# A relational graph layer on one core: root weight loaded early, features permuted early, basis parts in fours

## The reference, cut to what matters

```python
edge_index = jnp.stack([src, dst])
# layer 0: x @ W.T, normalised aggregation over edges, batch norm, GELU, + x
x = _layernorm(x + _L0_gnn_ref(x, edge_index, W, b, gamma, beta))
# layer 1, twice (relu between): w[r] = sum_b att[r,b] * basis[b]  (30 bases of 512x512)
w = jnp.einsum('rb,bio->rio', att, basis)
# gate = sigmoid(x_j @ gate_w[r]);  msg = (gate * x_j) @ w[type]
# out = segment_sum(msg) + x @ root + bias
x = _layernorm(x + _L1_gnn_ref(x, ...))
```

## Time and profile before

| | us |
|---|---|
| median of 3 runs (lowest, highest) | 323.28 (322.83, 325.36) |
| the profiled execution | 324.19 |
| its span | 322.2 |
| PE busy | 278.9 (87%) |
| DVE busy | 161.6 (50%) |
| ACT busy | 87.5 (27%) |
| POOL busy | 40.5 (13%) |
| basis matmuls (L495) busy | 65.8 |

### The profile page before, as it was taken

The page is one execution under the profiler, slowest core; times in us unless marked ns, Lnnn a source line. Parts: engine busy times, 40 slices in busy tenths (PEclk is TensorE's granted clock), DMA queues, the critical chain, the costliest instruction groups (busy, mean ns, idle before and its releaser), DMA issues.

```text
span 322.2 us, 4593 instructions
## 1 busy us (share of the span) xinstructions
PE 278.9 (87%) x1687; PEld 186.2 (58%) x1687; DVE 161.6 (50%) x362; ACT 87.5 (27%) x137; POOL 40.5 (13%) x76
## 2 busy tenths in 40 slices
PE   0797875989998796759999999999997999999991
PEld 0583332334565565217666656567775778778770
DVE  3888888885385745860620141342326125333333
ACT  5240203020155638543234024011313142100000
POOL 1001000000294005700000000000002700010000
PEclk9999999899899977978999999999999999999997
DMA  6992886589599996899996979876300500001112
GB/s 168 247 414 104 342 355 260 191 327 350 193 368 316 344 389 266 308 397 418 340 369 258 370 294 374 344 282 266 158 2 17 136 12 0 0 2 32 32 32 64
DMA packets 12803, 73.63 MB, mean 229 GB/s; under 512 B 2001, under 2 KB 2244, under 8 KB 4589
## 3 DMA queue, kind: packets, MB, share of 16 engines
q1 hardware_dynamic: 11330, 70.82, 58.3%
q0 software_dynamic: 1104, 2.36, 2.5%
q10 hardware_dynamic: 346, 0.17, 0.4%
HBM read 72.05 MB, written 1.28 MB: 228 GB/s over the span
## 4 chain that ended last, share of the span: by engine, by line
PE 67%; DVE 11%; DMA 8%; issue 5%; ACT 3%; POOL 2%; DVEq 2%; ACTq 0%; POOLq 0%
PE psW L495 16%; PE psM L476 9%; PE psM L478 9%; PE psM L477 9%; DMA basis_ring<-in_L_gnn_basis_dram 7%; PE psM L721 7%; PE psM L741 6%; PE psM L543 4%; DVE B L1038 3%; PE psE L576 3%; PE psM L619 2%; DVE oh_key L1045 2%; POOL root_lo L445 1%; DMA rows_i<-in_edge_type_dram 1%; DVE oh_src L1045 1%
## 5 line engine op out<-in xcount | busy, mean ns | idle before, releaser
L495 PE MATMUL psW<-basis_ring,S 128*32 128x512 f32 x512 | 65.8, 629 | 8.0 <-DMA basis_ring<-in_L_gnn_basis_dram 8.0
L1216 DVE SCALAR_TENSOR_TENSOR zg<-psM,gate,zg 125x512 fp32r<-125x512 f32 x20 | 15.0, 750 | 56.9 <-ACT zg L894 56.9
L495 PEld LDWEIGHTS psW<-basis_ring,S 128*32 128x32 f32 x512 | 13.6, 113 | 42.2 <-issue 29.9
L476 PE MATMUL psM<-w,hlT 128*125 128x512 f32 x80 | 32.4, 406 | 0.1
L478 PE MATMUL psM<-w,hlT 128*125 128x512 f32 x80 | 31.7, 396 | 0.0
L477 PE MATMUL psM<-w,hlT 128*125 128x512 f32 x80 | 31.6, 395 | 0.0
L576 PEld LDWEIGHTS psE<-oh_key,oh_src 128*125 128x125 f16 x162 | 14.5, 146 | 24.0 <-issue 19.3
L576 PE MATMUL psE<-oh_key,oh_src 128*125 128x160 f16 x162 | 17.4, 247 | 12.3 <-DVE B L1038 12.2
L894 ACT ACTIVATE zg<-psM,gate 125x512 fp32r<-125x512 f32 x20 | 13.8, 688 | 46.3 <-PE psM L478 45.9
L721 PEld LDWEIGHTS psM<-BB,zg 125*128 125x128 f32 x160 | 23.1, 188 | 3.4 <-issue 2.5
L721 PE MATMUL psM<-BB,zg 125*128 125x320 f32 (+1 forms) x160 | 24.1, 309 | 0.0
(11 more groups left out here) (152 smaller groups left out, 391.8 us busy)
## 6 DMA issues: line engine op xcount, KB each, us to landing
basis_ring<-in_L_gnn_basis_dram SPq DMA_DIRECT2D x64, 1024.0 KB, 6.8
root_raw<-in_L_gnn_root_dram POOLq DMA_DIRECT2D x32, 64.0 KB, 4.6
xs<-in_x_dram SPq DMA_DIRECT2D x1, 1120.0 KB
out_dram<-xs SPq DMA_DIRECT2D x5, 224.0 KB
w_raw<-in_L_gnn_W_dram SPq DMA_DIRECT2D x4, 256.0 KB, 9.5
bias_b<-in_L_gnn_bias_dram POOLq DMA_DIRECT2D x1, 250.0 KB, 3.7
xs<-in_x_dram SPq DMA_DIRECT2D x1, 130.0 KB
out_dram<-xs SPq DMA_DIRECT2D x5, 26.0 KB
```

The costliest lines, as they stand in the source:

```text
L476: nc.tensor.matmul(o, l_hi, r_hi, start=start, stop=False)
L495: m = nc.tensor.matmul(psW[32 * j:32 * j + 32, cc % 2, :], S[:, cc % 2, cc // CH, q].rearrange("p k r -> p (k r)"), ring[:, n % RING, j, : ...
L1216: link(v.scalar_tensor_tensor(out=zg[:, 1, c, r, :], in0=bank(("Z", L, c, r))[0:PC, :], scalar=gate[:, L, c, r:r + 1], in1=zg[:, 0, c, r, ...
```

## The change

- **Root weight 1, loaded early.** root1_raw gets a place of its own (it shares it with the combined-weight block 3, `w3`). SP issues its four loads of 256 KB right behind the first four basis loads and the vectors. ACT makes the high parts behind xw_out(4), once the first piece of AT is there; POOL makes low part 0 behind `diag` and one more behind each of the first three inverse roots of the batch norm. High and low parts lie where the one-hots were, which the combined-weight blocks 4 and 5 take after the root products; so `w_high(4)` and `w_first(5)` on ACT move behind all eight root outputs.
- **Features permuted early.** After the first transposes ACT permutes and doubles x in ten copies, through the place of the raw W. The residual sum becomes a plain sum.
- **diag** is one POOL instruction instead of five.
- **The loop of 27 groups** takes 18 parts (before 16) and all but two xw parts (before all but five); merge and low part of sum 0 come at groups 13 and 15 (before 16 and 19). The reads of the last four window places come ahead of their adds.
- **Parts 18 and 19** come before the degree sums (before: 16 to 19 behind them), the transposes of the small vectors behind them.
- **In the aggregation** the parts reach 21, 23, 27, 29, then 31 ahead of the GELU transposes, 33 behind them, 35 behind the second x1 transposes.
- **From the root products on** the marks are at the ends of sums (39, 43, 47, 51, 55, 59, 63): seven bursts of four parts, where there were fourteen of two (37, 39, ... 63).

```diff
         w_old = share([("oh_key", [P, OH, KEYS], F16), ("oh_src", [P, 3, G * P], F16),
                        ("key_pairs", [P, T, 2], F16), ("place_pairs", [P, T, 2], F16)],
-                      [("before_root1_raw", [P, KC, D], F32), ("root1_raw", [P, KC, D], F32)],
+                      [("root1_hi", [P, KC, D], F32R), ("root1_lo", [P, KC, D], F32R)],
                       [("w45", [P, 2, R, 2, D], F32R)])
-        oh_key, oh_src, key_pairs, place_pairs, root1_raw, w45 = (
-            w_old[n] for n in ("oh_key", "oh_src", "key_pairs", "place_pairs", "root1_raw", "w45"))
-        w03 = sb("w03", [P, 4, R, 2, D], F32R)
+        oh_key, oh_src, key_pairs, place_pairs, root1_hi, root1_lo, w45 = (
+            w_old[n] for n in ("oh_key", "oh_src", "key_pairs", "place_pairs", "root1_hi", "root1_lo", "w45"))
+        w02 = sb("w02", [P, 3, R, 2, D], F32R)
+        w_3 = share([("root1_raw", [P, KC, D], F32)], [("w3", [P, R, 2, D], F32R)])
+        root1_raw, w3 = w_3["root1_raw"], w_3["w3"]
...
-                      [("x_sum", [PC, NC, D], F32),
-                       ("root1_lo", [P, KC, D], F32R), ("root1_hi", [P, KC, D], F32R)],
+                      [("x_sum", [PC, NC, D], F32)],
...
+        use("deg", "dve")
         use("vec", "act")
-        use("deg", "dve")
...
-            return w03[:, b % WBLK] if b % WBLK < 4 else w45[:, b % WBLK - 4]
...
+            return w02[:, b % WBLK] if b % WBLK < 3 else w3 if b % WBLK == 3 else w45[:, b % WBLK - 4]
...
+        PARTS_IN = 17
...
-        MERGE_AT = {16: 0}
-        LOW_AT = {19: 0}
+        MERGE_AT = {13: 0}
+        LOW_AT = {15: 0}
...
+                    for j in range(JB):
+                        sp.dma_start(root1_raw[32 * j:32 * j + 32], root1.rearrange("(k c j) o -> j k c o", k=2 * KB, c=KC)[j]) \
+                            .then_inc(root1_in, 16)
...
             pool.wait_ge(dinv_ready, 1)
-            for c in range(NC):
-                nc.gpsimd.tensor_scalar(diag[:, c, :], ident[0:PC, 0:PC], dinv_p[:, c:c + 1], None, ALU.mult) \
-                    .then_inc(diag_ready, 1)
-
-            pool.wait_ge(at_ready, NC)
-            for kc in range(KC):
-                for j in range(JB):
-                    pool.dma_start(root1_raw[32 * j:32 * j + 32, kc],
-                                   root1.rearrange("(k c j) o -> c j k o", k=2 * KB, c=KC)[kc, j]) \
-                        .then_inc(root1_in, 16)
+            nc.gpsimd.tensor_tensor(diag[:], ident[0:PC, 0:PC].unsqueeze(1).broadcast_to([PC, NC, PC]),
+                                    dinv_p[:].unsqueeze(2).broadcast_to([PC, NC, PC]), ALU.mult).then_inc(diag_ready, 1)
+
+            def root1_low(k):
+
+                pool.wait_ge(root_hi, k + 1)
+                nc.gpsimd.tensor_tensor(in_q(root1_lo[:, k]), natural(root1_raw[:, k]), in_q(root1_hi[:, k].bitcast(F32)),
+                                        ALU.subtract).then_inc(root_ready, 1)
+
+            root1_low(0)
             for f in range(KC):
                 pool.wait_ge(var_ready, f + 1)
                 inverse_root(bn[:, 2, f:f + 1], 1)
-
-            def root1_low(k):
-
-                pool.wait_ge(root_hi, k + 1)
-                nc.gpsimd.tensor_tensor(in_q(root1_lo[:, k]), natural(root1_raw[:, k]), in_q(root1_hi[:, k].bitcast(F32)),
-                                        ALU.subtract).then_inc(root_ready, 1)
-
-            for k in range(KC - 1):
-                root1_low(k)
+                if f + 1 < KC:
+                    root1_low(f + 1)
             for c in range(NC):
                 pool.wait_ge(var_ready, KC + 1 + c)
                 link(nc.gpsimd.tensor_tensor(lrs[:, c:c + 1], lrs[:, c:c + 1], mhalf[0:PC, 0:1], ALU.pow))
                 nc.gpsimd.tensor_tensor(lnm[:, 1, c:c + 1], lnm[:, 0, c:c + 1], lrs[:, c:c + 1], ALU.mult) \
                     .then_inc(rstd_ready, 1)
-                if c == 1:
...
                     turn(i)
-                xw_upto(2 * (g - 3) // 3)
-                basis_upto(min(2 * g // 3 - 2, PARTS_IN))
+                xw_upto(3 * (g - 2) // 4)
+                basis_upto(min(3 * g // 4 - 1, PARTS_IN))
...
             xw_upto(NC * KC)
-            pe.wait_ge(vec_permuted, 1)
-            wait_free(pe, "vec")
-            for k in range(KC):
-                last[0] = nc.tensor.transpose(bank("vec")[:, k * NV:(k + 1) * NV], vec_rows_q[:, k * P:(k + 1) * P],
-                                              ident[0:NV, 0:NV])
-            done()
+            basis_upto(19)
             wait_free(pe, "deg")
             for s in range(NC):
                 pe.wait_ge(at_ready, s + 1)
@@ -605,9 +595,12 @@
                                                ones_r[:, 0:2], start=(s == 0 and c == 0),
                                                stop=(s == NC - 1 and c == NC - 1), skip_group_check=True)
             done()
-            basis_upto(17)
-
-            basis_upto(19)
+            pe.wait_ge(vec_permuted, 1)
+            wait_free(pe, "vec")
+            for k in range(KC):
+                last[0] = nc.tensor.transpose(bank("vec")[:, k * NV:(k + 1) * NV], vec_rows_q[:, k * P:(k + 1) * P],
+                                              ident[0:NV, 0:NV])
+            done()
 
...
-                        pe.wait_ge(diag_ready, NC)
+                        pe.wait_ge(diag_ready, 1)
...
-                basis_upto((21, 23, 25, 27)[f])
+                basis_upto((21, 23, 27, 29)[f])
+            basis_upto(31)
             for c in range(NC):
...
-            basis_upto(29)
+            basis_upto(33)
...
-                basis_upto((31, 33, 35)[c])
+                basis_upto((33, 35, 35)[c])
...
-                    basis_upto((37, 37, 39, 39, 41, 41, 43, 43)[KC * h + f])
+                    basis_upto((35, 39, 39, 39, 39, 43, 43, 43)[KC * h + f])
...
-                            basis_upto((45, 47, 47, 49, 51, 51, 53, 55, 55, 57)[R * c + r])
+                            basis_upto((43, 47, 47, 51, 51, 51, 55, 55, 59, 59)[R * c + r])
...
-                    basis_upto((57, 59, 59, 61, 61, 63, 63, 63)[KC * h + f])
+                    basis_upto((59, 59, 63, 63, 63, 63, 63, 63)[KC * h + f])
...
-                if pp == WBLK - 2:
-                    act.wait_ge(adj_used, T)
-                elif pp == WBLK - 1:
+                if pp == 3:
                     act.wait_ge(root_ready, KC)
+                elif pp in (WBLK - 2, WBLK - 1):
+                    act.wait_ge(main_full, uses[("root1", KC - 1, 1)] + 1)
                 elif pp >= WBLK:
...
             for i in range(len(turned)):
                 turned_out(i)
-            w_first(0)
+            act.wait_ge(main_full, uses[turned[-1]] + 1)
+            for c in range(NC):
+                x_q = w0_raw[0:PC, c % KC, :]
+                link(nc.scalar.activation(in_q(x_q), natural(xs[:, c, :]), ACT.Copy, scale=2.0))
+                link(nc.scalar.activation(xs[:, c, :], x_q, ACT.Copy))
+                if c == 1:
+                    w_first(0)
             xw_out(0)
             xw_out(1)
             w_high(0)
@@ -809,6 +809,10 @@
             xw_out(2)
             xw_out(3)
             xw_out(4)
+            act.wait_ge(root1_in, 16 * JB)
+            act.wait_ge(at_ready, 1)
+            for k in range(KC):
+                nc.scalar.activation(in_q(root1_hi[:, k]), natural(root1_raw[:, k]), ACT.Copy).then_inc(root_hi, 1)
             wait_full(act, "vec")
...
-            act.wait_ge(root1_in, 16 * KC * JB)
-            act.wait_ge(main_full, uses[("agg0", KC - 1, 1)] + 1)
-            for k in range(KC):
-                nc.scalar.activation(in_q(root1_hi[:, k]), natural(root1_raw[:, k]), ACT.Copy).then_inc(root_hi, 1)
-
...
-                    if (h, f) == (1, 1):
-                        w_high(4)
-                        w_first(5)
+
+            w_high(4)
+            w_first(5)
...
-            for w in range(NW - 4, NW):
-                add_window(w, window_at(w))
+            more = nc.values_load(more_i[0:1, 0:1], engines=[mybir.EngineType.DVE], min_val=0, max_val=N // W)
+            at = [window_at(w) for w in range(NW - 4, NW)]
+            for i, w in enumerate(range(NW - 4, NW)):
+                add_window(w, at[i])
             dve.wait_ge(win_added, NW)
 
-            more = nc.values_load(more_i[0:1, 0:1], engines=[mybir.EngineType.DVE], min_val=0, max_val=N // W)
...
-                link(v.scalar_tensor_tensor(out=in_q(x_sum[:, c, :]), in0=natural(xs[:, c, :]), scalar=2.0,
-                                            in1=in_q(bank(("g", c))[0:PC, :]), op0=ALU.mult, op1=ALU.add))
+                link(v.tensor_tensor(x_sum[:, c, :], xs[:, c, :], bank(("g", c))[0:PC, :], ALU.add))
                 dve.sem_inc(free_dve, 1)
```

12 lines of the change are left out of this document (5 added, 7 removed).

## The result

| us | before | after |
|---|---|---|
| median of 20 runs each (lowest, highest) | 324.51 (321.85, 328.35) | 320.82 (318.87, 323.55) |
| ratio, with its 95% interval | | 0.990 (0.987 to 0.992) |
| the profiled execution, its span | 324.19, 322.2 | 321.47, 319.3 |
| first root product | 144.71 | 140.38 |
| from there to the end of the span | 177.5 | 178.9 |

The ratios, here and in the table of the experiments, leave out executions in a slower state at a lower clock (five of ten of *e8*, one of four of *e16*, a few of the kernel before), which the medians hold.

The account below looks back on a forecast made before the run. Basis loads were taken to set the start of a solid 177.5 us block from the root products. Starting it 12.7 us earlier, less 0.8 for a longer block, gave 11.9 off 323.28: 311.4 us, range 306 to 318.5.

Parts of the forecast that it names:

- The root load at the front: Start of SP's queue: 1 MB ahead of basis loads 4 and 5 delays them some 5 us; cost nothing.
- The loop of 27 groups: Extra basis and xw parts cost nothing, covered by PE's waits for DVE; at most 4.5 us without that cover.
- The tail: End of the loop: window registers read before the adds save 0.5 us (bounds nothing and 1.9); AT whole at 82.5.
- The degree sums 0.6 behind AT: On PE after the loop: sums end at 83.1 instead of 85.95, 2.9 us earlier.
- z 6.4 behind the sums: Way over DVE, POOL and ACT after the degree sums: z whole at 89.5, where it was 92.33.
- Third aggregation block at 101.2: Third of four aggregation blocks starts then instead of 105.34: 3.0 us earlier, plus 1.1 of load wait gone.
- middle stretch does not start earlier: Rival: idle PE before z at half clock, or a longer loop, loses the 3.0 us and more; 315 us, chance 0.14.
- The chain of loads: Middle stretch: load 28 issued at 106.4, then loads 2.5 us apart, part 35 landing at 128.5.
- Where it comes from: Main effect, part 35 landing 14.3 us earlier: root weight gone, ring refilled before the stretch, parts 30 and 31 filling GELU wait.
- Behind the GELU: From GELU transposes through x1 transposes and DVE's low parts: root products start at 132.0 instead of 144.71, 12.7 us earlier.
- The block, +0.8: From the root products on: seven bursts of four gain 1.4 us in shape changes, lose 2.2 in two load waits.
- fours starve: Rival: in the block behind the root products, load waits of 5.5 us and slow-clock stretches; 318 us, chance 0.15.

Follow-up runs that it names:

- e8: Kernel before with the bursts of four parts from the root products on and nothing else; 327.48 us, ratio 1.005.
- e16: Kernel before with only the changed middle marks for basis parts (21 to 35); 325.42 us, ratio 1.011.
- e12: Kernel after with the root weight alone put back as before; 315.72 us, ratio 0.973.
- e4: Kernel after with POOL's low part 0 moved behind the first inverse root, each low part following its inverse root; 317.55 us, ratio 0.980.
- e1: Kernel after with the root weight's loads issued behind basis load 11 instead of load 3; 319.07 us, ratio 0.986.
- e2: Kernel after with pairs instead of fours behind the root products; 319.48 us, ratio 0.988.
- e3: Kernel after with parts 18 and 19 moved behind the degree sums and vector transposes; 319.06 us, ratio 0.987.
- e11: Kernel after with e1, e10, e3, e4 and e5 together; 313.94 us, ratio 0.967.
- e18: Kernel before with the new schedule of all parts up to 35 (front and middle marks) and nothing else; 316.95 us, ratio 0.977.
- e17: Kernel before with the new schedule of basis parts up to 19 alone; 318.23 us, ratio 0.980.
- e10: Kernel after with pairs instead of fours, the first pair one root product later; 317.58 us, ratio 0.981.
- e13: Kernel after with e12, e10, e3 and e5 together; 315.36 us, ratio 0.974.
- e5: Kernel after with the last four window places read between the adds again; 320.84 us, ratio 0.988.
- e14: Kernel before with the features permuted early and nothing else; 324.82 us, ratio 1.003.

## Why the prediction missed

**The root load at the front, "nothing".** This step failed. The prediction let 1 MB stand ahead of loads 4 and 5 in the queue and held that the ring does not need them until then. It did not look up when parts 4 and 5 are taken: with the denser parts of the loop that is 34 and 36 us. The loads landed 10.2 and 11.9 us behind their issue; in e12 it was 4.5 and 6.5. The loop of 27 groups, likewise "nothing", is 2.7 us longer by DVE's one-hots, of which PE waits 2.4 and is then at half clock. With the low part of the same weight beside z (below) this is what *e12* takes away, 5 us by the medians. The two more parts and three more xw parts are not the cause: e12 has them too, and its loop is 57.9 us. The cover held; the queue did not.

**The tail, −0.5.** It was +0.95. The bounds were nothing and a gain of 1.9; that the reads could do more harm in one go than between the adds was left out. A bound on the other side was there to be had: the adds between the reads were in a place where DVE waited for PE anyway. AT starts at 82.99 and not at 78.8: 2.7 + 1.45 + 0.1 for the first one-hot = 4.2.

**The degree sums 0.6 behind AT.** Right, with 0.8: AT ends at 86.68, the sums at 87.45.

**z 6.4 behind the sums.** 7.4: the one instruction of 2.01 us beside POOL's low part, a term that the prediction did not have. It priced low part 0 by POOL's own time (behind diag, nothing queued) and not by what DVE does then. With it away (e4, e12) it is 6.2. ACT's root_hi did end in time, at 87.88, as forecast.

**Third aggregation block at 101.2.** 107.86. From the end of z it is 13.0 us, 11.7 were forecast: PE at half clock from 88.3 to 98.5. This is the rival "middle stretch does not start earlier", with both of its conditions, the idle PE in front of z and the longer loop. I gave it 0.5 to 1 us beyond the lost 3.0 and a chance of 0.14. From AT's start to the second aggregation block it is 19.0 us, and it was 18.9: all that the change wins by opening this chain, the clock and the low part take back.

The clock was in the rows already. The prediction read one 8 early in the clock row; there are two, and the second is the 11th slice, in front of z. There the kernel before was at half clock for 3.4 us, and its parts 16 to 19 took 5.34 us, not the 3.7 that the prediction gives four parts. No wait stood ahead of that, only the degree sums. The same fall is in eighteen of the nineteen traces (e16 has none). In six of them (e1, e2, e3, e4, e11, e18) the clock falls while the sums still run and before any wait for z. PE in e4, sums from 83.35 to 87.38, and then in the kernel before, behind them:

```profile
83.35:85.75 2.40, 2.37 (x18) 1.00 0.91 280
85.80:87.30 1.50, 1.50 (x8) 0.50 0.91 366
```
```profile
86.70:90.00 3.30, 3.30 (x20) 0.50 0.52 174
```

So the fall comes with the degree sums, whatever stands behind them; whether PE then idles goes with its length, up to 6.8 us in the runs with parts taken there and 6.8 to 10.2 in those without. The rival named the idling alone.

**The chain of loads, 22.1 us from the issue of load 28 to the landing of load 35.** Right to 0.1 us: 113.4 to 135.6, where 106.4 to 128.5 was forecast. Both ends are 7 us late, as the stretch is.

**Where it comes from.** The prediction named the root weight being gone, the ring refilled, and the GELU wait filled. The second and the third are right (e17, e18). The first is wrong: e12 has the root weight in its old place on POOL and loads just as quickly. It was slow beside loads 20 to 25 only because these were issued late. The earlier trace rows could not tell the two apart; the change moved both, and I gave the credit to the wrong one.

**Behind the GELU.** The transposes of x1 come 5.8 us behind those of the GELU (5.5), the root products 13.0 (12.6). Part 31 is done at 127.4; its records took 1.81 us at half clock, behind two waits for parts 30 and 31 of 1.05 and 1.42. So 7.0 us late by the issue of load 28, 1.0 by this, and 0.4 by the steps behind it make up the 8.4. The 7.0 are the terms above: 4.2 at AT's start, 1.2 until z is whole, 1.3 at the third aggregation block, 0.3 from there to the load.

**The block, +0.8.** +1.4. The waits are 4.3 us in four bursts, where 2.2 in two were forecast (1.26, 1.25, 0.27, 1.48). The changes of shape: 178.9 − 4.3 = 174.6 us against 177.5, of which about 1.5 is the half clock at the first root products before (records 0.27 us apart, not 0.15, for 3.3 us); 1.4 is left for seven bursts, as forecast. Two comparisons without that correction give 2.1 each: e10 (176.7) against 174.6, and before (177.5) against e8 without its waits (179.1 − 3.7). The rival "fours starve" (5.5) and the forecast (2.2) lie on either side of the 4.3 us of waits, and the rival was wrong in the clock: waits of 1.5 us and less in this block are not followed by a slow stretch. "TensorE: Matmul & The Clock Gate" of the Trainium skill (section "HAM oscillation — how this bites in real kernels") warns of short bursts with waits between them; the trace agrees at parts 4 and 5 and at parts 30 and 31, where waits of 0.94 and 1.42 us and of 1.05 and 1.42 us, one part apart, end in 3.4 us at half clock each, and not in the block. It does not agree in every run either: *e13* waits 0.96 and 1.40 us for parts 30 and 31 and stays at full clock, *e12* waits 1.42 and 1.41 and does not.

**The range.** Its upper end, 318.5, let one rival happen at a time. What happened is the middle rival (315) with its sizes doubled, and part of the starving one. The loop's bound of 4.5 us was written down and left out of the range. (The case of more gain, 307.5, is 307.8 by its own terms, 311.4 − 1.4 − 2.2.)

## What to carry to other kernels

When a change moves a transfer and the order of what runs beside it, the trace of before cannot say which of the two was at fault; look at when the neighbours were issued, and look for a hole in the queue. Here the best place for a 1 MB weight was 9 us of empty queue made by taking four tiles earlier, and not the front of the program, where the next tile in the ring paid for it. Price every piece of "hidden" work also by what the other engines do in those microseconds: a term on an idle engine cost the busy one 1.3 us. And compare more than one profiled execution before you give a size: here the same edit cost the loop between 0.5 and 4.7 us.

## What the runs showed of the hardware that I had not expected

- An elementwise instruction of 125 x 512 on DVE took 2010 ns instead of 740 while POOL ran a 128 x 512 subtraction of 1.97 us (1.53 elsewhere); without it the longest was 930. It is so in all six runs with the two side by side.
- Five register reads on DVE in one go are 2.97 us of standing still, some 0.6 us each; one each between dependent adds leaves gaps of 0.43 to 0.51.
- Basis loads of 1 MB issued behind another 1 MB in one queue landed 10.2 and 11.9 us behind their issue, 4.5 and 6.5 without it. In the kernel before, loads beside 16 loads of 64 KB on another queue needed up to 14.2 (load 25).
- PE's granted clock was at half (1.2 GHz) for 10.2 us, 88.3 to 98.5. It fell 0.5 us into a wait of 3.3 us, behind 3.5 us of degree sums; in six other runs it fell while such sums ran, before the wait for z.
- A wait of 0.9 to 1.8 us and one of 1.4, with one basis part (1.07 us) between them, were followed by 3.4 us at half clock in some runs (after, e4 and e5 at parts 4 and 5; after, e5 and e12 at parts 30 and 31) and not in others (e13 and e1 at parts 30 and 31). Four waits of up to 1.5 us between dense products in the block left the clock at full speed, and one of 1.67 us there was followed by 3.4 us at half clock in two of nineteen runs (e13, e14).
